# Fourteen late normalisations of a projection, spread over three pairs of heads, their low halves on GpSimd, and the output weights loaded and split in another order

## The chip, the cores and the metric

The kernel runs on one core of one Trainium2 chip. The metric is the device time of one execution in microseconds (us), the median of several runs. The engines of the core are TensorE (PE), VectorE (DVE), ScalarE (ACT), GpSimd (POOL) and SyncE (SP), which issues all DMAs. Each engine works through its own instruction list in order; semaphores make one wait for another.

## The reference

One transformer layer on x of shape (4, 512, 512): a batch of B = 4 sequences of T = 512 tokens. 32 query heads and 8 key/value heads of size 64, a sliding window of 256, and then a gated feed-forward part. All is float32.

```
xq = _rms_norm(x @ wq.T, q_norm_w, EPS)      # 2048 columns: 32 heads
xk = _rms_norm(x @ wk.T, k_norm_w, EPS)      # 512 columns: 8 heads
xv = x @ wv.T
...
scores = einsum('bhtd,bhsd->bhts', xq, xk) * scale + bias[None]   # bias: alibi slope * distance, -inf outside the window
attn = softmax(scores)
out = einsum('bhts,bhsd->bhtd', attn, xv)
return out @ wo.T
...
x = x + _layernorm(attention(_layernorm(x)))
x = x + _layernorm(feed_forward(_layernorm(x)))
```

## The kernel before

Matrix products are done on split operands: a float32 value is kept as a high half (rounded) and a low half (the rest), and a product is the sum of three. So each tensor that TensorE reads needs a rounding (ScalarE, a copy into the high half) and a subtraction (the low half).

**Stage 1, projections.** Four batches one after another. For a batch there are 16 blocks of query rows and 4 of key rows, 128 rows by 512 tokens each, numbered f = 0 to 19 (f 16 to 19 are the keys), kept in `raw[:, f]`. A block is normalised in three steps: VectorE scales it by its weight and the inverse root (line 927, `raw<-raw,norm_w,inv_rms`), ScalarE rounds it into `qk[:, f % 4, 0]` (line 731), VectorE subtracts (line 922, `split_raw`) into `qk[:, f % 4, 1]`. SP then stores the block to `q_scr` or `k_scr` (`store_qk`, line 385). The first LATE = 6 blocks are normalised in the batch's own time; the other 14 (f 6 to 19) are late: those of batches 0 to 2 are done during the next batch, those of the last batch during the first part of stage 2.

**Stage 2, attention.** 16 pairs n of key/value heads, four pairs to a batch. A pair is 32 units u: two key/value heads (u 0 to 15, and 16 to 31), four query tiles of 128 tokens in each, four query heads in each tile. The window of a tile is 128, 256, 384 and 384 wide, so units 0 to 3 and 16 to 19 are narrow, 4 to 7 and 20 to 23 are 256 wide, the rest 384. The stages of a unit run on a software pipeline whose lags stand in `LAGS`. In step u, VectorE does the subtraction for the transposed probabilities of unit u - 3 (line 997, `pT_lo`), then adds the bias to the scores of unit u (line 990, `u_sb`); ScalarE takes the exponentials of unit u (line 794) and rounds the transposed probabilities of unit u - 2 (line 802); TensorE makes scores (1231), transposes (1240) and the products with the values (1256 to 1258). Once for a group of four units (group g of a pair is units 4g to 4g+3), VectorE inverts the sums (line 1005, in step 4g+4) and takes the group's result out of PSUM into `o_raw` (line 1011, in step 4g+8).

GpSimd finishes a group (`finish_o`): it multiplies by the inverse sums into `o_mid` (line 598) and by the norm of v into `o_out` (line 604), which SP stores to `o_scr` (`store_o`, line 414). GpSimd also builds the next bias tile (`make_bias`, line 588), two for a pair. `o_raw` and `inv_sum` are rings of two, so VectorE waits before the inversion and the taking of a group until `o_mid` of the group two earlier is done:

```
def invert_sums(n, u):
    a = 2 * TT * n + u // REP
    dve.wait_ge(p_ready, UNITS * n + u + 1)
    at_least(dve, o_mid_ready, a - 1)
```

In pair 0, units 0 to 13 are each followed by one late normalisation of the last batch: in the loop of each engine, `norm(B - 1, u + LATE)` stands behind the unit's work, where VectorE scales block u + 6 and subtracts block u + 5, and ScalarE rounds block u + 5.

In pairs 1 to 4 the output weights are brought in: SP loads a quarter of them (1 MB, `load_wo`, line 433), and GpSimd rounds and subtracts four chunks of it (`split_wo`, lines 612 and 615), one behind groups 1 and 2 each and one behind groups 4 and 5 each. From pair 5 on each pair also carries one tile of the output projection: SP loads the tile (`load_o`, line 420) once the stores of the four pairs before have landed, and TensorE transposes it from step 4 on.

The order of all work is written out by hand, the same for each engine: `attention_loops` calls `attend(n)` for the 16 pairs, pair 0 and pair 5 written out, the others in loops of the engines.

## Time and profile before

| what | value |
|---|---|
| median of 3 runs | 1305.19 us (1304.18 to 1307.57) |
| the profiled execution's own time | 1309.66 us |
| its span in the trace | 1307.9 us |
| mean granted clock of TensorE, share of full speed | 0.973 |
| busy: PE, DVE, ACT, POOL | 93%, 73%, 58%, 28% of the span |

The median is of runs without a profile. The profiled execution is one run of its own; its time is the span plus 1.8 us that lie around it. In rows of busy time by stretch, the columns are: the stretch (us from the span's start), its length, busy us and count of instructions for PE, PE's weight loads (PEld), DVE, ACT and POOL, then the granted clock of TensorE (1.00 is 2.4 GHz, 0.50 is 1.2 GHz), the busy share of the DMA engines, and GB/s. In rows of a timeline the columns are: start in us, length in us, engine, line, operation, operands with their shapes, count, and in square brackets the idle time before it and what ended it. Matmul ends are modelled, so a busy PE need not be a PE at its peak.

### The profile page before, as it was taken

What the parts mean: (1) busy time and instruction counts of PE and PEld (TensorE: products, weight loads), DVE (VectorE), ACT (ScalarE), POOL (GpSimd) and SP (SyncE); (2) the same over time, 40 slices, a digit from 0 to 9 for tenths busy, and PEclk for the clock granted to TensorE, in tenths of its full rate; (3) what the DMA queues carried; (4) which work ended last, traced back from release to release, by engine and by line L of the source; (5) the groups of instructions that cost most, each with busy time, mean ns of one, the idle gap of its engine ahead of it and who ended that gap; (6) DMA issues with size and microseconds to landing.
All of it is one profiled execution on the core that took longest, in us unless ns stands there. A gap on an engine that the chain in (4) does not pass through costs nothing.

```text
span 1307.9 us, 30500 instructions
## 1 busy us (share of the span) xinstructions
PE 1214.9 (93%) x9016; PEld 1019.5 (78%) x9016; DVE 954.1 (73%) x2528; ACT 761.1 (58%) x2013; POOL 369.1 (28%) x445
## 2 busy tenths in 40 slices
PE   5999999996699998999999999999989979999998
PEld 4868777784577777898888888888877768888876
DVE  4597776858889987888888888888864346546464
ACT  3545455554589887777877777777732234232330
POOL 1000000001147766445354444434421100202021
PEclk9999999997599998999999999999989989999999
DMA  4216262455555556455454554545352252101010
GB/s 155 103 73 242 114 240 113 193 213 186 232 178 170 168 168 197 130 187 166 155 181 148 187 163 154 174 152 186 126 183 97 88 185 81 65 33 65 33 65 34
DMA packets 99245, 189.03 MB, mean 145 GB/s; under 512 B 8032, under 2 KB 36832, under 8 KB 99168
## 3 DMA queue, kind: packets, MB, share of 16 engines
q1 hardware_dynamic: 99168, 188.07, 42.2%
q8 instruction: 40, 0.66, 0.2%
q14 instruction: 37, 0.30, 0.1%
HBM read 116.48 MB, written 71.57 MB: 144 GB/s over the span
## 4 chain that ended last, share of the span: by engine, by line
PE 63%; DVE 12%; issue 10%; DMA 6%; ACT 4%; POOL 3%; SPq 1%; DVEq 1%; POOLq 0%; ACTq 0%
PE bank L1209 17%; PE bank L1340 15%; PE bank L1277 12%; PE bank L1240 6%; PE bank L1231 6%; DVE u_sb L990 3%; DMA wo_stage<-woT 2%; PE bank L1266 2%; DVE pT_lo L997 2%; DVE inv_rms L944 2%; ACT p_sb L794 1%; PE bank L1256 1%; PE bank L1258 1%; PE bank L1257 1%; DMA o_in<-o_scr 1%
## 5 line engine op out<-in xcount | busy, mean ns | idle before, releaser
L794 ACT ACTIVATE p_sb<-u_sb,low 128x384 f32<-128x384 f32 (+2 forms) x512 | 273.8, 535 | 84.6 <-DVE low L990 57.3
L990 DVE CUSTOM_DVE_ANT_0 u_sb<-bank,bias 128x384 f32<-128x384 f32 (+2 forms) x512 | 231.5, 452 | 40.5 <-PE bank L1231 21.0
L1231 PE MATMUL bank<-k_st,q_st 128*128 128x384 f32 (+2 forms) x1024 | 252.9, 329 | 6.5 <-DVE v_out L964 2.9
L1240 PE MATMUL bank<-ident,p_sb 128*128 128x128 f32 x1152 | 225.6, 287 | 31.4 <-DVE pT_lo L997 23.1
L997 DVE TENSOR_TENSOR pT_lo<-bank,pT_hi 128x384 f16<-128x384 f32 (+2 forms) x512 | 232.0, 453 | 28.9 <-ACT pT_hi L802 18.0
L802 ACT ACTIVATE pT_hi<-bank 128x384 f16<-128x384 f32 (+2 forms) x512 | 204.2, 399 | 49.5 <-PE bank L1240 47.7
L1231 PEld LDWEIGHTS bank<-k_st,q_st 128*128 128x128 f32 x1024 | 178.7, 195 | 30.3 <-DVE low L990 4.3
L1240 PEld LDWEIGHTS bank<-ident,p_sb 128*128 128x128 f32 x1152 | 139.8, 143 | 78.0 <-ACT p_sb L794 40.1
L598 POOL TENSOR_TENSOR o_mid<-o_raw,inv_sum 128x256 f32<-128x256 f32 x128 | 82.9, 648 | 285.1 <-DVE o_raw L1011 283.8
L561 POOL TENSOR_TENSOR rstd<-var_eps,minus_half 128x1 f32<-128x1 f32 (+1 forms) x31 | 23.4, 754 | 492.1 <-DVE var_eps L888 492.1
L1256 PE MATMUL bank<-v_st,pT_hi 128*128 128x64 f16 x1152 | 156.9, 195 | 0.5 <-DVE pT_lo L997 0.5
L1257 PE MATMUL bank<-v_st,pT_hi 128*128 128x64 f16 x1152 | 156.7, 194 | 0.0
L1258 PE MATMUL bank<-v_st,pT_lo 128*128 128x64 f16 x1152 | 156.7, 194 | 0.0
L1340 PE MATMUL bank<-zT_hi,gu 128*128 128x512 f32 x352 | 139.5, 396 | 0.6 <-DVE hid L1125 0.6
L1340 PE MATMUL bank<-zT_lo,gu 128*128 128x512 f32 x352 | 138.2, 393 | 0.0
L1209 PE MATMUL bank<-xT_hi,w_hi 128*128 128x512 f32 x320 | 127.5, 398 | 4.5 <-DVE xT_lo L906 4.5
L1209 PE MATMUL bank<-xT_hi,w_lo 128*128 128x512 f32 x320 | 125.1, 391 | 0.0
L1209 PE MATMUL bank<-xT_lo,w_hi 128*128 128x512 f32 x320 | 125.1, 391 | 0.0
L1277 PE MATMUL bank<-wo_hi,oT_hi 128*128 128x512 f32 x256 | 110.3, 431 | 8.9 <-DVE oT_lo L1016 8.9
L588 POOL TENSOR_TENSOR bias<-dist,slopes 128x1536 f32<-128x1536 f32 x33 | 91.1, 2762 | 87.5 <-PE bank L1209 87.5
L1256 PEld LDWEIGHTS bank<-v_st,pT_hi 128*128 128x128 f16 x1152 | 113.8, 101 | 1.7 <-DVE pT_lo L997 0.7
L1257 PEld LDWEIGHTS bank<-v_st,pT_hi 128*128 128x128 f16 x1152 | 107.5, 99 | 6.6
(114 smaller groups left out, 2416.5 us busy)
## 6 DMA issues: line engine op xcount, KB each, us to landing
...
o_scr<-o_out SPq DMA_DIRECT2D x128, 128.0 KB, 2.7
...
```

What stands on the lines that cost most here:

```text
L794: nc.scalar.activation(p_sb[:, u % RING, 0:w], u_sb[:, u % RING, 0:w], ACT.Exp, scale=-1.0, bias=low[:, u % RING:u % RING + 1], accum_out= ...
L802: nc.scalar.activation(pT_hi[:, u % RING, 0:w], bank[2 + u % 2][:, 0:w], ACT.Copy).then_inc(pT_hi_ready, 1)
L990: nc.vector.tensor_tensor_reduce(out=u_sb[:, u % RING, 0:w], in0=bank[u % 2][:, 0:w], in1=bias[:, 2 * u // UNITS, u % REP, at:at + w], sca ...
L997: nc.vector.tensor_tensor(pT_lo[:, u % RING, 0:w], bank[2 + u % 2][:, 0:w], pT_hi[:, u % RING, 0:w], ALU.subtract).then_inc(pT_ready, 1)
L1209: mm = nc.tensor.matmul(bank[n % 4][:], lhs, rhs, start=(kc == 0 and k == 0), stop=(kc == KC - 1 and k == 2))
L1231: mm = nc.tensor.matmul(bank[u % 2][:, 0:w], q_st[:, s, r, P * i:P * i + P], k_st[:, s, part, P * key:P * key + w], start=(part == 0), sto ...
L1240: mm = nc.tensor.transpose(bank[2 + u % 2][:, P * j:P * j + P], p_sb[:, u % RING, P * j:P * j + P], ident[:])
L1256: nc.tensor.matmul(acc, hi, v_hi, start=(j == 0), stop=False, skip_group_check=True)
L1257: nc.tensor.matmul(acc, hi, v_lo, start=False, stop=False, skip_group_check=True)
L1258: mm = nc.tensor.matmul(acc, lo, v_hi, start=False, stop=(j == tiles - 1), skip_group_check=True)
L1277: mm = nc.tensor.matmul(acc[:], lhs, rhs, start=(chunk == 0 and k == 0), stop=(chunk == QC - 1 and k == 2))
L1340: mm = nc.tensor.matmul(acc, lhs, rhs, start=(first and k == 0), stop=(last and k == len(products) - 1))
```

## The change

The 14 late blocks of the last batch move from units 0 to 13 of pair 0 to units 2, 4, 6, 18 and 20 of pairs 0, 1 and 2: f 6 to 10 in pair 0, f 11 to 15 in pair 1, f 16 to 18 at units 2, 4, 6 and f 19 at unit 18 of pair 2. VectorE keeps only the scaling (`scale_raw`). ScalarE rounds a block one unit later. The subtraction goes to GpSimd (`split_late`): for the blocks of a pair's first half it stands behind the bias of the second head and ahead of group 0, for those of the second half behind the next pair's bias and ahead of group 4. SP stores the late blocks in pieces (`store_late`), and the load of output weights is issued ahead of the pair's late stores. Two of the four splits of output weights in a pair move from behind groups 1 and 2 to behind groups 2 and 3. Pairs 1 to 4 are written out in place of a loop of the engines.

```
+LATE_UNITS = (2, 4, 6, 18, 20)
+LATE_NORMS = {}
+for _k, _f in enumerate(range(LATE, QC + KVC)):
+    LATE_NORMS[_k // len(LATE_UNITS), LATE_UNITS[_k % len(LATE_UNITS)]] = _f
+
+def late_norms(n, first, end):
+    return [LATE_NORMS[n, u] for u in LATE_UNITS if isinstance(n, int) and first <= u < end and (n, u) in LATE_NORMS]
...
 def attention_loops(eng, attend):
-    attend(0)
-    with eng.Fori(1, LAG) as n:
+    for n in range(LAG):
         attend(n)
...
 # SP
+            def store_late(n, first, end):
+                for f in late_norms(n, first, end):
+                    store_qk(B - 1, f)
+                    if f == QC + KVC - 1:
+                        stage1_stored(B)
...
                 load_heads(n, 0)
                 store_o(n - 1, 0, [TT - 1])
+                if isinstance(n, int):
+                    store_late(n - 1, UNITS // 2, UNITS)
...
                 if wo:
                     load_wo(n - 1)
+                if isinstance(n, int):
+                    store_late(n, 0, UNITS // 2)
                 store_o(n, 0, [0])
...
-            for f in range(LATE, QC + KVC):
-                store_qk(B - 1, f)
-            stage1_stored(B)
+            store_late(0, 0, UNITS // 2)
             store_o(0, 0, range(TT - 1))
-            with sp.Fori(1, LAG) as n:
+            for n in range(1, LAG):
                 attend(n, wo=True)
...
 # GpSimd
+            def split_late(n, first, end):
+                for f in late_norms(n, first, end):
+                    pool.wait_ge(qk_hi_ready, (QC + KVC) * (B - 1) + f + 1)
+                    pool.wait_ge(qk_ready, (QC + KVC) * (B - 1) + f)
+                    nc.gpsimd.tensor_tensor(out=qk[:, f % QK_RING, 1], in0=raw[:, f], in1=qk[:, f % QK_RING, 0].bitcast(F32),
+                                            op=ALU.subtract).then_inc(qk_ready, 1)
...
                 make_bias(n, q, 1)
+                split_late(n, 0, UNITS // 2)
                 for i in range(TT):
                     finish_o(n, q, 0, i)
-                    if wo and i in (1, 2):
-                        split_wo(n - 1, i - 1)
+                    if wo and i in (2, 3):
+                        split_wo(n - 1, i - 2)
...
                 make_bias(n + 1, q + 1, 0)
+                split_late(n, UNITS // 2, UNITS)
                 for i in range(TT // 2):
                     finish_o(n, q, 1, i)
...
 # ScalarE
-                    if isinstance(n, int) and n == 0 and u + LATE < QC + KVC:
-                        norm(B - 1, u + LATE)
+                    if isinstance(n, int) and n == 0 and u == 0:
+                        round_raw(B - 1, LATE - 1)
+                    for f in late_norms(n, u - 1, u):
+                        round_raw(B - 1, f)
...
 # VectorE
-                    if isinstance(n, int) and n == 0 and u + LATE < QC + KVC:
-                        norm(B - 1, u + LATE)
+                    if isinstance(n, int) and n == 0 and u == 0:
+                        split_raw(B - 1, LATE - 1)
+                    for f in late_norms(n, u, u + 1):
+                        scale_raw(B - 1, f)
```

The next rows are the instruction list of VectorE in pair 0, from the bias of unit 3 on, before the change. The `ISA` rows are the bias addition and the reading of its minimum; `pT_lo` is the subtraction of unit u - 3.

```order
L990 ISA u_sb,low<-bank,bias 128x128
L990 ISA low 128x1
L927 SCALAR_TENSOR_TENSOR raw<-raw,norm_w,inv_rms 128x512
L922 TENSOR_TENSOR qk<-raw,qk 128x512
L997 TENSOR_TENSOR pT_lo<-bank,pT_hi 128x128
L990 ISA u_sb,low<-bank,bias 128x256
L990 ISA low 128x1
L1005 RECIPROCAL inv_sum<-p_sum 128x4
L927 SCALAR_TENSOR_TENSOR raw<-raw,norm_w,inv_rms 128x512
L922 TENSOR_TENSOR qk<-raw,qk 128x512
L997 TENSOR_TENSOR pT_lo<-bank,pT_hi 128x128
L990 ISA u_sb,low<-bank,bias 128x256
```

The same place after the change:

```order
L1026 ISA u_sb,low<-bank,bias 128x128
L1026 ISA low 128x1
L1033 TENSOR_TENSOR pT_lo<-bank,pT_hi 128x128
L1026 ISA u_sb,low<-bank,bias 128x256
L1026 ISA low 128x1
L1041 RECIPROCAL inv_sum<-p_sum 128x4
L959 SCALAR_TENSOR_TENSOR raw<-raw,norm_w,inv_rms 128x512
L1033 TENSOR_TENSOR pT_lo<-bank,pT_hi 128x128
L1026 ISA u_sb,low<-bank,bias 128x256
L1026 ISA low 128x1
L1033 TENSOR_TENSOR pT_lo<-bank,pT_hi 128x128
L1026 ISA u_sb,low<-bank,bias 128x256
```

Each unit had a scaling and a subtraction of a late block; now unit 3 has neither and unit 4 has a scaling only.

The list of GpSimd in the loop of pairs 1 to 4 before, from the bias of the second head (`bias`) over groups 0 and 1 to the first split of output weights (`REGISTER_ALU` and `ISA` rows are loop arithmetic):

```order
L588 TENSOR_TENSOR bias<-dist,slopes 128x1536
L595 REGISTER_ALU
L598 TENSOR_TENSOR o_mid<-o_raw,inv_sum 128x256
L146 ISA
L604 ISA
L604 TENSOR_TENSOR o_out<-o_mid,v_norm 128x256
L595 REGISTER_ALU
L598 TENSOR_TENSOR o_mid<-o_raw,inv_sum 128x256
L604 TENSOR_TENSOR o_out<-o_mid,v_norm 128x256
L610 REGISTER_ALU
L612 ISA
L612 COPY wo_hi<-wo_stage 128x512
```

The list of GpSimd in pair 1 after, from the same bias on:

```order
L607 TENSOR_TENSOR bias<-dist,slopes 128x1536
L642 TENSOR_TENSOR qk<-raw,qk 128x512 x3
L617 TENSOR_TENSOR o_mid<-o_raw,inv_sum 128x256
L623 TENSOR_TENSOR o_out<-o_mid,v_norm 128x256
L617 TENSOR_TENSOR o_mid<-o_raw,inv_sum 128x256
L623 TENSOR_TENSOR o_out<-o_mid,v_norm 128x256
L617 TENSOR_TENSOR o_mid<-o_raw,inv_sum 128x256
L623 TENSOR_TENSOR o_out<-o_mid,v_norm 128x256
L631 CAST wo_hi<-wo_stage 128x512
L634 TENSOR_TENSOR wo_lo<-wo_stage,wo_hi 128x512
L617 TENSOR_TENSOR o_mid<-o_raw,inv_sum 128x256
L623 TENSOR_TENSOR o_out<-o_mid,v_norm 128x256
```

Three subtractions of late blocks (`qk<-raw,qk`) stand between the bias and group 0, and the split of output weights, which stood behind group 1, stands behind group 2.

The list of SyncE behind the last load of the projections before, over pair 0 and up to its leaving of pair 0:

```order
L385 DMA q_scr<-qk 128x1024
L467 DMA v_norm<-vn_scr 128x512
L468 DMA v_norm<-vn_scr 128x128
L385 DMA q_scr<-qk 128x1024 x10
L385 DMA k_scr<-qk 128x1024 x4
L414 DMA o_scr<-o_out 128x256 x3
```

The same place after, down to the last store ahead of the load of output weights (`k_st`, `q_st`, `v_st` are the loads of a head):

```order
L395 DMA q_scr<-qk 128x1024 x3
L424 DMA o_scr<-o_out 128x256 x3
L408 DMA k_st<-k_scr 64x1024 x2
L410 DMA q_st<-q_scr 128x4x512
L412 DMA v_st<-v_scr 128x512
L424 DMA o_scr<-o_out 128x256
L395 DMA q_scr<-qk 128x1024 x2
L424 DMA o_scr<-o_out 128x256 x3
L408 DMA k_st<-k_scr 64x1024 x2
L410 DMA q_st<-q_scr 128x4x512
L412 DMA v_st<-v_scr 128x512
L424 DMA o_scr<-o_out 128x256
```

All 14 late stores stood ahead of the first store of an attention result; now 3 of them do, 2 stand between stores and head loads, and the load of output weights (`wo_stage`) comes next, with 5 of the 14 issued.

## Rows read from the trace of the kernel before

**Rows 1.** The page of the profile, part 1: busy time, share of the span and instructions by engine.

```profile
PE 1214.9 (93%) x9016; PEld 1019.5 (78%) x9016; DVE 954.1 (73%) x2528; ACT 761.1 (58%) x2013; POOL 369.1 (28%) x445
```

**Rows 2.** Busy time by engine in pair 0 (its two halves), pair 2 and pair 4; columns as named in section 3.

```profile
319.16:357.77 38.61, 24.24 (x134) 17.99 (x135) 31.69 (x81) 21.67 (x61) 3.86 (x4) 0.50 0.66 255
357.77:374.50 16.73, 16.35 (x189) 13.50 (x188) 14.33 (x57) 13.95 (x48) 8.05 (x9) 0.94 0.51 156
...
406.32:438.18 31.86, 30.40 (x356) 24.63 (x354) 29.26 (x113) 28.59 (x97) 22.98 (x26) 1.00 0.53 173
...
471.24:505.14 33.90, 31.41 (x363) 26.25 (x362) 29.43 (x113) 28.41 (x95) 23.61 (x27) 0.95 0.50 159
```

**Rows 3.** Timeline of VectorE in pair 0, units 8 and 9: start, length, line, operands, [idle before].

```profile
337.44 0.55 DVE L990 CUSTOM_DVE_ANT_0 u_sb<-bank,bias 128x384 f32<-128x384 f32 x1
...
340.34 0.54 DVE L990 CUSTOM_DVE_ANT_0 u_sb<-bank,bias 128x384 f32<-128x384 f32 x1
340.81 0.08 DVE L990 DVE_READ_ACCUMULATOR2_ANT low<- 128x1 f32 x1
...
342.18 0.69 DVE L922 TENSOR_TENSOR qk<-raw,qk 128x512 fp32r<-128x512 f32 x1 [0.63 <-ACT qk L731]
```

**Rows 4.** Timeline of VectorE in pair 2: first operation of units 4, 8, 12, 16.

```profile
409.86 0.43 DVE L990 CUSTOM_DVE_ANT_0 u_sb<-bank,bias 128x256 f32<-128x256 f32 x1
...
413.26 0.55 DVE L990 CUSTOM_DVE_ANT_0 u_sb<-bank,bias 128x384 f32<-128x384 f32 x1
...
417.62 0.55 DVE L990 CUSTOM_DVE_ANT_0 u_sb<-bank,bias 128x384 f32<-128x384 f32 x1
...
422.14 0.28 DVE L990 CUSTOM_DVE_ANT_0 u_sb<-bank,bias 128x128 f32<-128x128 f32 x1
```

**Rows 5.** Timeline of TensorE in pair 0: transposes of two units in succession, clock at half.

```profile
355.76 0.87 PE L1240 MATMUL bank<-ident,p_sb 128*128 128x128 f32 x3 [1.38 <-DVE pT_lo L997]
...
357.39 0.86 PE L1240 MATMUL bank<-ident,p_sb 128*128 128x128 f32 x3
```

**Rows 6.** Two microseconds in which the clock of TensorE rises; columns as in group 2.

```profile
358.00:360.00 2.00, 2.00 (x26) 1.89 (x23) 1.33 (x7) 0.96 (x4) 1.21 (x2) 0.56 0.23 71
```

**Rows 7.** Timeline of GpSimd at the end of the projections.

```profile
296.85 5.90 POOL L588 TENSOR_TENSOR bias<-dist,slopes 128x1536 f32<-128x1536 f32 x2 [87.54 <-PE bank L1209]
```

**Rows 8.** Timeline of VectorE at the same time.

```profile
300.06 3.23 DVE L956 TENSOR_TENSOR sum_sq<-sum_sq,square 128x512 f32<-128x512 f32 x1
```

**Rows 9.** Line 956 of VectorE over the whole span: shortest, median and longest duration in ns.

```profile
L956 DVE TENSOR_TENSOR sum_sq<-sum_sq,square x72: 682/692/3228, 28.7 to 300.1; 128x512 f32<-128x512 f32 x72
```

**Rows 10.** Timeline of GpSimd in pairs 1 and 2.

```profile
394.65 0.61 POOL L612 CAST wo_hi<-wo_stage 128x512 f32 x1
395.51 1.28 POOL L615 TENSOR_TENSOR wo_lo<-wo_stage,wo_hi 128x512 f32 x1 [0.25 <-POOL wo_hi L612]
396.75 0.61 POOL L598 TENSOR_TENSOR o_mid<-o_raw,inv_sum 128x256 f32<-128x256 f32 x1
...
398.26 2.75 POOL L588 TENSOR_TENSOR bias<-dist,slopes 128x1536 f32<-128x1536 f32 x1
...
412.34 2.75 POOL L588 TENSOR_TENSOR bias<-dist,slopes 128x1536 f32<-128x1536 f32 x1
```

**Rows 11.** Timeline of GpSimd in pair 4: the first split of the fourth load.

```profile
489.52 0.61 POOL L612 CAST wo_hi<-wo_stage 128x512 f32 x1 [4.41 <-DMA wo_stage<-woT]
```

**Rows 12.** Timeline of VectorE in pairs 4 and 5: two long waits.

```profile
492.26 0.18 DVE L1005 RECIPROCAL inv_sum<-p_sum 128x4 f32<-128x4 f32 x1 [1.52 <-POOL o_mid L598]
...
511.45 0.42 DVE L990 CUSTOM_DVE_ANT_0 u_sb<-bank,bias 128x256 f32<-128x256 f32 x1 [1.99 <-PE bank L1231]
```

**Rows 13.** Timeline of SyncE's DMA issues around the start of pair 5.

```profile
493.87 1.17 SPq L398 DMA_DIRECT2D k_st<-k_scr  x2
...
496.77 0.35 SPq L414 DMA_DIRECT2D o_scr<-o_out  x1
504.17 0.38 SPq L420 DMA_DIRECT2D o_in<-o_scr  x1
```

More of the change, by code:

```diff
@@ L646, in _ @@
             make_bias(0, 0, 1)
+            split_late(0, 0, UNITS // 2)
             pool.wait_ge(vn_loaded, 2 * DMA)
@@ L650, in _ @@
             make_bias(1, 1, 0)
+            split_late(0, UNITS // 2, UNITS)
             for i in range(TT // 2):
                 finish_o(0, 0, 1, i)
-            with pool.Fori(1, LAG) as n:
+            for n in range(1, LAG):
                 attend(n, n, wo=True)
@@ L922, in split_raw, with scale_raw @@
                 nc.vector.tensor_tensor(qk[:, f % QK_RING, 1], raw[:, f], qk[:, f % QK_RING, 0].bitcast(F32), ALU.subtract).then_inc(qk_ready, 1)
-            def norm(b, f):
+            def scale_raw(b, f):
                 dve.wait_ge(inv_ready, 2 * b + f // QC + 1)
@@ L928, in norm @@
                                                ALU.mult, ALU.mult).then_inc(scaled, 1)
+            def norm(b, f):
+                scale_raw(b, f)
                 if f:
```

## The prediction

> **What bounds the kernel now.** I read the page first, then the timelines of VectorE and ScalarE where the late blocks lie, and then busy time cut at the first bias addition of each pair. TensorE is busy 93% of the span [rows 1], but the cut shows a place where it is not. The first 16 units of pair 0 take 38.61 us, with the granted clock at 0.50 (1.2 GHz) throughout and TensorE busy 24.2 us of them; the next 16 units take 16.73 us at 0.94. Pair 2, with no late blocks, takes 31.86 us at 1.00, with VectorE busy 29.3 and ScalarE 28.6 of it; pair 4 takes 33.90 [rows 2]. Pair 3, which lies between the end of pair 2 at 438.18 and the start of pair 4 at 471.24, takes 33.06.
>
> Why pair 0 is slow stands in its timeline. Unit 8 starts at 337.44 and unit 9 at 340.34, a period of 2.90 us. In it VectorE adds the bias, scales a block (0.74), then stands idle 0.63 us for ScalarE's rounding (`ACT qk L731`) before it subtracts (0.69) [rows 3]. ScalarE can't round earlier, since its exponential for the unit is ahead. So it is a serial round trip for each block. The same eight units 8 to 15 in pair 2 take 422.14 - 413.26 = 8.88 us, 1.11 each [rows 4]. TensorE starves meanwhile and its clock stays at the lower level.
>
> Three later places matter. In pair 4, GpSimd waits 4.41 us for the load of output weights, with group 2 queued behind the split; VectorE then stands 1.52 us at an inversion of sums that needs `o_mid` [rows 11, 12]. At step 5 of pair 5 VectorE stands 1.99 us for TensorE, which is waiting for `o_in`, whose load was issued at 504.17 [rows 12, 13].
>
> **The change, part by part.** All in us. An offset is a time from a pair's first bias addition.
>
> *Pair 0, first half: from 38.6 to about 22.* Eleven of 14 scalings and 14 of 15 subtractions leave it, and with them the round trips; block 5's subtraction at unit 0 stays, with its wait. Units 1 to 7 become narrow units with three scalings. What limits them is TensorE at half clock: two successive sets of transposes, with three sets of value products and one 128-wide pair of scores between, start 357.39 - 355.76 = 1.63 apart [rows 5]. Scaled by width, I estimate 0.85 for a 128-wide unit, 1.3 for a 256-wide one and 1.9 for a 384-wide one (1.63 plus the wider scores). Unit 0, 2.0; units 1 to 3 with a scaling, 3.3; units 4 to 7 with two, 5.7: unit 8 at 11.0 to 11.5. Before, it came at 337.44 - 319.16 = 18.3. Units 8 to 15 take 8.9 at full clock. TensorE had been without long waits from 355.8 when the clock rose between 358 and 360 [rows 5, 6], so I expect it back within two units of unit 8, at 0.8 extra each: 10.5. Sum 22, a gain of 16.6; the ends are 26.5 (clock down to unit 16, 1.9 each) and 19.5.
>
> *Pair 0, second half: from 16.7 to 17.6.* The cold start, 0.9, goes (15.8 in pair 2: 422.14 - 406.32); two scalings come, 0.66 each (0.74 long, less the 0.07 or 0.08 by which an operation overlaps the next: 340.34 + 0.54 against 340.81 [rows 3]), and 0.5 for collisions on GpSimd. Net for pair 0: -15.7.
>
> *Scalings in pairs 1 and 2: +5.9.* Nine at 0.66. VectorE and ScalarE are each some nine tenths busy there, so a scaling lands on the path; the rounding (0.5) lies beside it on ScalarE. The lower bound is nothing, if waits of VectorE take it in; the upper is the 1.6 it cost in pair 0 ((38.61 - 15.8) / 14).
>
> *A scaling that meets GpSimd: +4.7 over pairs 1 and 2.* A scaling reads two SBUF operands, as does line 956, which lasts 0.69 in the median but 3.23 once, at 300.06, just when GpSimd ran two bias tiles from 296.85 to 302.75 [rows 7 to 9]. It ended 0.54 behind the second tile. So one waits for the other to finish. The Trainium skill's page "SBUF — State Buffer", section "SBUF: two separate sides", has it as an exclusive lock between GpSimd and a VectorE operation with two SBUF inputs; by this rule the trace agrees, and it speaks against this change. By the row the sum below is -8.0; if the row of 3.23 had another cause it would be -12.7. Where do they meet? GpSimd's bias of the second head started at 412.34, offset 6.0, and lasts 2.75 [rows 10]. With two scalings ahead of it the bias runs from 6.7 to 9.4, and the scaling of unit 6 comes at about 7.4: 2.0 of wait. The bias additions and `pT_lo` read PSUM and are not held. The other scalings meet shorter work, 0.2 each or so: 2.4 in pair 1, 2.3 in pair 2.
>
> *GpSimd's queue: +2.4.* A split of output weights costs 396.75 - 394.65 = 2.10, its subtraction of the late blocks' size 1.28, a group 398.26 - 396.75 = 1.51, a bias 2.75 [rows 10]. Pair 1 needs 2 x 2.75 + 8 x 1.51 + 4 x 2.10 + 5 x 1.3 = 32.5 of GpSimd in about 38. It fits, but not everywhere. Behind the taking of group 3 (step 20) now stand group 3, a split, a bias, two subtractions and `o_mid` of group 4: 1.5 + 2.1 + 2.75 + 2.6 + 0.8 = 9.8. VectorE wants that `o_mid` at the inversion in step 28. Steps 20 to 28 take 417.62 - 409.86 = 7.76 (of the same widths) [rows 4] and one scaling: 8.4. VectorE stands some 1.5 in pair 1; in pair 2, with one subtraction and no scaling there, 0.9. In pair 0 there is no split and no wait. In the first half of a pair the same sum with three subtractions is 1.5 + 2.75 + 3.9 + 0.8 = 9.0 against 7.8 + 1.3 + the 2.0 of the lock, so nothing more. Ends: 0, and 6 if the lock delays GpSimd too.
>
> *Pairs 3 to 5: -5.3.* The first split now comes behind group 2, at offset 15.8 + 2.7 = 18.5; the weights landed at 489.52 - 471.24 = 18.3 at the latest [rows 11]. GpSimd's wait, and VectorE's, go: pair 3 from 33.06 and pair 4 from 33.90 to 31.85, 3.3 in all. Group 2 of pair 4 is then finished some 3 us earlier, so head loads (issued 493.87, 22.6 into the pair, where step 20 of pair 2 comes near 19.4 by the same steps [rows 4]) and the store that the load of `o_in` waits for (496.77) go out that much earlier, and `o_in` lands near step 4 of pair 5: I take 2.0 off. Lower bound none, if that store's 7.2 us behind the head loads are what counts.
>
> *Moved or added at nothing.* Late stores: 0.5 MB each, 14 of them, in pairs where DMA engines are half busy [rows 2]; head loads have 12 units of lead. A store ahead of a group's store makes that up to 2 us later, with a ring of four in `o_out`. Pairs 1 to 4 written out: pair 0 was so already, and a loop's turn shows no gap to gain.
>
> Sum: -15.7 + 5.9 + 4.7 + 2.4 - 5.3 = -8.0. From the profiled execution's 1309.66 that is 1301.7; that run lies 4.5 above the median of 1305.19, so for a median I forecast 1297.2.
>
> **The rivals.**
>
> *GpSimd is hardly felt* (0.16). Lock and queue cost 1, since VectorE's delays slide past GpSimd's work: -15.7 + 5.9 + 1 - 5.3 = -14, 1291. For it: the schedule leaves GpSimd 5 us in pair 1. Against: the bias lies just where unit 6's scaling comes.
>
> *The gain is given back* (0.20). The clock stays low to unit 16 (+4.5), and stalls in pairs 1 and 2 cost 3 more with a short spell at half clock, as in pair 4 (0.95 there [rows 2]): -0.5 to -3, 1303. For it: with TensorE busy 24.2 of 38.6 us, 63%, the clock did not rise [rows 2].
>
> *Slower, by the lock* (0.08). If each of the nine scalings of pairs 1 and 2 meets a bias or a split and waits 2 us or more on average, these pairs cost 5.9 + 18 + 2.4 = 26.3, against 15.7 and 3.3 (with `o_in` not better): +7, 1312. It decides from 1.9 us of average wait on. Against: GpSimd's operations other than bias last 0.6 to 1.3 [rows 10].
>
> *The forecast* (0.56): -4 to -12, 1293 to 1301.
>
> **How the numbers follow.** Within 0.3% (3.9 us) is what a measurement of this kernel can't tell from none. Faster takes the forecast's and the first rival's chance, 0.72; same the second, 0.20; slower 0.08. The range leaves out the slower case and a tenth at the low end: 1288 to 1305.
>
> **What the profile will show.** Right: unit 16 of pair 0 about 22 us after unit 0, the clock at 1.00 from about unit 10; a scaling of 2.7 us beside a bias tile in pairs 1 and 2; an inversion waiting for `o_mid` in step 28 of pair 1; pairs 1 and 2 near 39.4 and 37.8 (6 to 7.6 more); pair 4 at 31.9. Wrong: a clock at 0.50 to the end of pair 0, a wait at a group other than 4, pairs of 34 (no lock) or above 42, or `o_in` landing as late as before.

## The result and the profile after

The changed kernel takes 1291.52 us in the median (1289.15 to 1292.30), the kernel before 1306.38 in runs of the same session: a ratio of 0.9876, 95% interval 0.9859 to 0.9893. The ratios in this document are estimates over the single runs of both kernels, and not exactly the quotient of two medians, which is 0.9886 here. By the medians the change takes 14.9 us off. The forecast was 1297.2; the forecast, too, was below the time before, but by 8.0. The profiled executions are 1309.66 and 1292.3, and their spans 1307.9 and 1290.5.

The page's busy time by engine, to be held against [rows 1]: VectorE has lost 10.0 us, GpSimd has gained 20.3, and TensorE has the same instructions at a higher mean clock (0.989 after, 0.973 before).

```profile
PE 1202.0 (93%) x9016; PEld 1009.0 (78%) x9016; DVE 944.1 (73%) x2514; ACT 758.4 (59%) x2013; POOL 389.4 (30%) x459
```

Busy time of the changed kernel, cut at the first bias addition of each pair (the two halves of pair 0, then pairs 1 to 5), which answers to [rows 2]:

```profile
317.01:334.36 17.35, 15.31 (x145) 12.51 (x146) 15.32 (x57) 15.08 (x49) 6.81 (x7) 0.83 0.72 255
334.36:351.51 17.15, 15.43 (x179) 12.24 (x178) 15.59 (x60) 15.16 (x51) 10.95 (x11) 1.00 0.60 193
351.51:389.26 37.75, 30.93 (x355) 24.48 (x354) 32.88 (x118) 30.73 (x102) 29.27 (x29) 1.00 0.62 214
389.26:425.12 35.86, 30.97 (x356) 24.64 (x354) 31.98 (x117) 30.37 (x102) 30.30 (x31) 1.00 0.61 214
425.12:456.09 30.97, 30.12 (x353) 24.41 (x352) 28.60 (x112) 28.13 (x97) 23.12 (x27) 1.00 0.55 180
456.09:487.41 31.32, 30.32 (x355) 24.54 (x354) 28.78 (x113) 28.24 (x97) 23.35 (x27) 1.00 0.57 184
487.41:527.67 40.26, 39.35 (x413) 35.39 (x412) 34.10 (x121) 32.41 (x102) 18.91 (x21) 1.00 0.59 189
```

| length of | before | forecast | after |
|---|---|---|---|
| pair 0, units 0 to 15 | 38.61 | 22 | 17.35 |
| pair 0, units 16 to 31 | 16.73 | 17.6 | 17.15 |
| pair 1 | 31.82 | 39.4 | 37.75 |
| pair 2 | 31.86 | 37.8 | 35.86 |
| pair 3 | 33.06 | 31.85 | 30.97 |
| pair 4 | 33.90 | 31.85 | 31.32 |
| pair 5 | 42.32 | 40.3 | 40.26 |

Summed over the table the change takes 17.6 us off. Pair 6 gives back 0.4 (41.20 to 41.62) and pairs 7 to 14 another 0.4. Pair 0 starts 2.15 earlier in the profile of after; in the profiles of the other kernels below it starts anywhere from 316.70 to 318.98 with nothing changed ahead of it, so that is not the change's. Behind the start of pair 15, where no kernel here differs, 1.6 are lost (390.05 before, 391.67 after). So from the start of pair 0 to the end of the span the two profiles differ by 15.2. The stretch behind the start of pair 15 takes 388.28 to 391.67 in the fourteen profiles, and it tends to be shorter where the clock of TensorE stood at 1.2 GHz for less of it: up to the last 3 us of the span that is 10.2 us in e6's profile (388.35), 13.7 in before's and 17.1 in after's. Spans of single profiles can therefore differ by up to 3.4 us for this alone, and the kernels below are compared by the lengths of their pairs and by medians.

**Pair 0.** The clock of TensorE in stretches of 2 us from the span's 318 on:

```profile
318.00:320.00 2.00, 1.02 (x6) 0.70 (x5) 1.62 (x6) 1.03 (x5) 0.00 (x0) 0.50 0.99 354
320.00:322.00 2.00, 2.00 (x15) 1.87 (x14) 1.87 (x9) 1.98 (x8) 0.31 (x1) 0.50 1.04 347
322.00:324.00 2.00, 2.00 (x17) 1.80 (x16) 1.99 (x8) 1.71 (x7) 1.36 (x2) 0.76 1.05 276
324.00:326.00 2.00, 1.63 (x19) 1.13 (x19) 1.86 (x9) 1.93 (x8) 1.21 (x1) 1.00 1.02 383
```

TensorE is busy without a gap in the second and third rows, at 1.2 GHz, and goes to 2.4 GHz inside the third: at unit 6, not two units behind unit 8. Unit 8 starts at 8.23 (forecast 11.0 to 11.5), and units 8 to 15 take 9.12 (forecast 10.5).

**Pairs 1 and 2.** VectorE (first fence) and GpSimd (second fence) in these pairs:

```profile
357.74 0.96 DVE L959 SCALAR_TENSOR_TENSOR raw<-raw,norm_w,inv_rms 128x512 f32<-128x512 f32 x1
...
366.08 0.18 DVE L1041 RECIPROCAL inv_sum<-p_sum 128x4 f32<-128x4 f32 x1 [1.06 <-POOL o_mid L617]
...
385.19 0.18 DVE L1041 RECIPROCAL inv_sum<-p_sum 128x4 f32<-128x4 f32 x1 [1.45 <-POOL o_mid L617]
...
403.66 0.18 DVE L1041 RECIPROCAL inv_sum<-p_sum 128x4 f32<-128x4 f32 x1 [1.07 <-POOL o_mid L617]
...
420.89 0.18 DVE L1041 RECIPROCAL inv_sum<-p_sum 128x4 f32<-128x4 f32 x1 [0.83 <-ACT p_sb L825]
```

```profile
356.22 1.00 POOL L617 TENSOR_TENSOR o_mid<-o_raw,inv_sum 128x256 f32<-128x256 f32 x1 [2.16 <-DVE o_raw L1047]
357.42 0.73 POOL L623 TENSOR_TENSOR o_out<-o_mid,v_norm 128x256 f32<-128x256 f32 x1 [0.20 <-DVE low L1026]
358.10 3.20 POOL L607 TENSOR_TENSOR bias<-dist,slopes 128x1536 f32<-128x1536 f32 x1
361.27 4.13 POOL L642 TENSOR_TENSOR qk<-raw,qk 128x512 fp32r<-128x512 f32 x3
365.35 0.62 POOL L617 TENSOR_TENSOR o_mid<-o_raw,inv_sum 128x256 f32<-128x256 f32 x1
...
384.46 0.62 POOL L617 TENSOR_TENSOR o_mid<-o_raw,inv_sum 128x256 f32<-128x256 f32 x1
...
420.17 0.61 POOL L617 TENSOR_TENSOR o_mid<-o_raw,inv_sum 128x256 f32<-128x256 f32 x1
```

The scaling of unit 6 starts 0.36 ahead of the bias tile, and the tile doesn't hold it: it ends 2.60 ahead of the tile's end. What holds it a little, to 0.96 in place of 0.75, is the `o_out` that began at 357.42. There are four waits for `o_mid`, at steps 12 and 28 of each pair: an inversion starts 0.11 behind the end of each `o_mid` shown. The last wait is named after ScalarE, but `o_mid` ends at 420.78, and the inversion follows by the same 0.11. The waits add up to 1.06 + 1.45 + 1.07 + 0.83 = 4.4. I had forecast 1.5 and 0.9 at the two steps 28, and nothing at the two steps 12.

**Pairs 3 to 5.** GpSimd's first split of pair 4, and SyncE's issues around it, which answer to [rows 11, 13]:

```profile
474.37 0.61 POOL L631 CAST wo_hi<-wo_stage 128x512 fp32r<-128x512 f32 x1 [0.15 <-DMA wo_stage<-woT]
```

```profile
474.61 1.12 SPq L408 DMA_DIRECT2D k_st<-k_scr  x2
...
484.95 0.38 SPq L430 DMA_DIRECT2D o_in<-o_scr  x1
```

The 4.41 of waiting in pair 4 became 0.15. Head loads go out 18.5 into the pair (before: 22.6), and the load of `o_in` 2.46 ahead of pair 5 (before: 0.97).

### The profile page after: what moved, and what is told of

Its sections match the earlier page's. It is cut to its first block, busy times and chain, and to the rows that moved or that the text cites. A ratio compares the mean times of both kernels' runs of the same rounds, so it can differ in the third digit from the quotient of the medians.

```text
span 1290.5 us, 29717 instructions
## 1 busy us (share of the span) xinstructions
PE 1202.0 (93%) x9016; PEld 1009.0 (78%) x9016; DVE 944.1 (73%) x2514; ACT 758.4 (59%) x2013; POOL 389.4 (30%) x459
## 4 chain that ended last, share of the span: by engine, by line
PE 70%; DVE 12%; issue 8%; ACT 4%; POOL 3%; DMA 2%; DVEq 0%; ACTq 0%; POOLq 0%; SPq 0%
PE bank L1247 17%; PE bank L1378 17%; PE bank L1315 12%; PE bank L1278 8%; PE bank L1269 7%; DVE u_sb L1026 3%; ACT p_sb L825 2%; PE bank L1294 2%; PE bank L1304 2%; PE bank L1296 2%; PE bank L1295 2%; DVE pT_lo L1033 2%; DVE inv_rms L980 2%; POOL bias L607 1%; POOL qk L642 1%
## 5 line engine op out<-in xcount | busy, mean ns | idle before, releaser
L1269 PE MATMUL bank<-k_st,q_st 128*128 128x384 f32 (+2 forms) x1024 | 247.2, 323 | 4.4 <-DVE v_out L1000 2.9
L1278 PE MATMUL bank<-ident,p_sb 128*128 128x128 f32 x1152 | 220.9, 282 | 29.1 <-DVE pT_lo L1033 19.2
L1269 PEld LDWEIGHTS bank<-k_st,q_st 128*128 128x128 f32 x1024 | 175.4, 191 | 27.7 <-DVE v_out L1000 3.3
L1278 PEld LDWEIGHTS bank<-ident,p_sb 128*128 128x128 f32 x1152 | 137.1, 141 | 75.9 <-ACT p_sb L825 49.9
L1294 PE MATMUL bank<-v_st,pT_hi 128*128 128x64 f16 x1152 | 154.7, 193 | 0.5 <-DVE pT_lo L1033 0.5
L1295 PE MATMUL bank<-v_st,pT_hi 128*128 128x64 f16 x1152 | 154.9, 193 | 0.0
L1294 PEld LDWEIGHTS bank<-v_st,pT_hi 128*128 128x128 f16 x1152 | 112.3, 100 | 1.7 <-DVE pT_lo L1033 0.7
L1295 PEld LDWEIGHTS bank<-v_st,pT_hi 128*128 128x128 f16 x1152 | 105.9, 98 | 5.8
```

Of the source, the lines that this page charges most:

```text
L1269: mm = nc.tensor.matmul(bank[u % 2][:, 0:w], q_st[:, s, r, P * i:P * i + P], k_st[:, s, part, P * key:P * key + w], start=(part == 0), sto ...
L1278: mm = nc.tensor.transpose(bank[2 + u % 2][:, P * j:P * j + P], p_sb[:, u % RING, P * j:P * j + P], ident[:])
L1294: nc.tensor.matmul(acc, hi, v_hi, start=(j == 0), stop=False, skip_group_check=True)
L1295: nc.tensor.matmul(acc, hi, v_lo, start=False, stop=False, skip_group_check=True)
```

## The experiments

All times are medians; each ratio is to the kernel before, timed in the same session. Lengths of pairs and single instructions are from one profile of each kernel.

| kernel | us | ratio, 95% interval |
|---|---|---|
| changed | 1291.52 | 0.9876 [0.9859, 0.9893] |
| e1 written out | 1303.42 | 0.9970 [0.9955, 0.9984] |
| e2 and split order | 1300.45 | 0.9955 [0.9939, 0.9971] |
| e3 spread, subtraction on VectorE | 1308.36 | 1.0007 [0.9997, 1.0017] |
| e4 pair 0 only, subtraction on GpSimd | 1300.84 | 0.9953 [0.9937, 0.9970] |
| e5 old split order | 1291.71 | 0.9884 [0.9865, 0.9903] |
| e6 groups ahead of late blocks | 1287.13 | 0.9848 [0.9828, 0.9869] |
| e7 scaling meets bias | 1293.72 | 0.9898 [0.9880, 0.9917] |
| e8 GpSimd's subtraction cut | 1285.95 | 0.9841 [0.9821, 0.9861] |
| e9 VectorE's scaling cut | 1285.70 | 0.9842 [0.9823, 0.9861] |
| e10 splits behind 2, 4, 5, 6 | 1287.89 | 0.9859 [0.9836, 0.9882] |
| e11 group 0 ahead only | 1289.22 | 0.9868 [0.9845, 0.9892] |
| e12 six, four, four | 1287.20 | 0.9848 [0.9826, 0.9870] |

### e1 and e2: the other parts of the change, alone

To the kernel before, e1 does only this, on each engine (GpSimd's lines are shown), and e2 adds the order of the splits:

```
-            with pool.Fori(1, LAG) as n:
+            for n in range(1, LAG):
...
 # e2 as well
-                    if wo and i in (1, 2):
-                        split_wo(n - 1, i - 1)
+                    if wo and i in (2, 3):
+                        split_wo(n - 1, i - 2)
```

> The kernel before, with pairs 1 to 4 written out in place of a loop, and nothing else. The trace of the changed kernel has pairs 3 and 4 at 31.0 and 31.3 us, less than the 31.8 of pair 2 before, where no wait stood to be removed. Theory A: a written-out pair is 0.5 to 0.9 us shorter than one in a loop, so 2 to 3.5 us less than before. Theory B (my prediction's): a loop costs nothing, the kernel is at before's time, and what pairs 3 and 4 gained is all from the order of the splits.

> As the run before it, and two of the four splits of output weights behind groups 2 and 3 in place of 1 and 2. The late blocks stay as before. Theory A: the waits of GpSimd for the load and of VectorE for o_mid in pairs 3 and 4 go (3.3 us), and o_in is in time in pair 5 (2 us): 5 us less than the written-out kernel, 7 to 8.5 less than before. Theory B: only the split waits go and pair 5 still waits for its load, 3 us less than the written-out kernel.

Pair 4 of e1, and of e2:

```profile
466.67:500.88 34.21, 31.20 (x355) 26.30 (x354) 29.23 (x113) 28.72 (x97) 24.04 (x29) 0.95 0.50 163
```

```profile
465.55:497.03 31.48, 30.34 (x355) 24.57 (x354) 28.82 (x113) 28.29 (x97) 23.26 (x27) 1.00 0.64 207
```

Pairs 1 to 4 take 130.64 before (374.50 to 505.14 [rows 2]), 128.96 in e1 and 125.02 in e2. So writing out brings 1.7 there, where I had nothing, and the split order 3.9, where I had 3.3 for the waits. Pair 2, in which VectorE waits for no `o_mid` in either kernel, is 31.86 before and 31.13 in e1. Only some of this is the same in each pair: the first four units take 3.30 in all four pairs of e1, and 3.43 to 3.55 before. Pair 1 falls by 0.2 alone, and pair 4 grows by 0.3, since GpSimd waits 4.90 there for the weights and VectorE 2.05 for `o_mid`. Pair 5, which is not in the loop, falls from 42.32 to 41.01 in e1: its `o_in` is issued 1.55 ahead of the pair, where it was 0.97. e2 brings it to 40.39. So a part of what I had put down to the split order comes with the writing out. Which instructions of the loop cost the time was not taken apart. In both kernels theory A came, in e1 with somewhat more than its 2 to 3.5. In e1 the clock falls in pair 4 as it did before; in e2, with the wait gone, it doesn't.

### e3: the spread without GpSimd

The changed kernel, with the subtraction on VectorE two units behind the scaling:

```
-                split_late(n, 0, UNITS // 2)
...
+                    for f in late_norms(n, u - 2, u - 1):
+                        split_raw(B - 1, f)
```

> The changed kernel, with the 14 late blocks spread the same way but the subtraction kept on VectorE, two units behind the scaling, so that the rounding is done by then. Theory A: 14 subtractions at 0.6 us cost VectorE 8.4, of which the three waits for o_mid in pairs 1 and 2 (1.06, 1.45 and 1.07 us) are given back: 4 to 5 us slower than the changed kernel, 1296. Theory B: GpSimd's share is a loss, through its queue and the shared port: not slower than the changed kernel, 1291 or less.

This kernel has all other parts of the change, those of e2 with them. Against e2's 1300.45 the spread with VectorE's subtractions costs 7.9: pairs 0 to 2 take 40.85, 43.60 and 39.33, 123.8 together, against 117.4 in e2 (55.08, 31.12, 31.19) and 108.1 in the changed kernel. What pair 0 gains, 14.2, pairs 1 and 2 lose and more, 20.6. The spread by itself does most of the work where it was meant to: the first half of pair 0 takes 20.03 here, 38.61 before and 17.35 in the changed kernel. But with the subtractions on VectorE, where this kernel puts them, pairs 1 and 2 lose it all again. Neither theory had this: A expected 4 to 5 us over the changed kernel, and it is 17. In pair 1 VectorE (first fence) meets GpSimd (second), and TensorE starves (third, a stretch of 4 us):

```profile
366.39 2.11 DVE L943 TENSOR_TENSOR qk<-raw,qk 128x512 fp32r<-128x512 f32 x1 [0.65 <-ACT qk L750]
```

```profile
365.21 2.75 POOL L607 TENSOR_TENSOR bias<-dist,slopes 128x1536 f32<-128x1536 f32 x1
```

```profile
366.00:370.00 4.00, 2.10 (x11) 1.56 (x11) 3.61 (x6) 1.51 (x6) 1.95 (x1) 0.50 1.03 337
```

A subtraction of 0.69 takes 2.11, and TensorE, busy 2.10 of 4.00 us, stands at 1.2 GHz. The clock had already fallen at 365.09, ahead of this meeting, and it falls once in each half of pairs 1 and 2. The subtraction also waits 0.65 for its rounding, so the round trip is not gone either. How much of the 20.6 is the subtractions' own length, how much the meetings and how much the clock isn't separated, and a place for them on VectorE that is clear of GpSimd was not tried.

### e4: GpSimd without the spread

The kernel before, with the 14 blocks where they were and their subtractions on GpSimd:

```
-                        norm(B - 1, u + LATE)
+                        norm(B - 1, u + LATE, late=True)     # VectorE: scaling only
...
+            split_late(range(6, 13))                         # GpSimd, ahead of group 0
...
+                split_late({0: range(13, 17), 1: range(17, 20)}.get(i, ()))
```

> The kernel before, with all 14 late blocks in units 0 to 13 of pair 0, but the subtraction on GpSimd; loop and order of splits as before. Theory A: the cost in pair 0 is the round trip from VectorE over ScalarE back to VectorE, so that without it a unit falls from 2.9 us to TensorE's 1.9 at half clock: 10 to 12 us less than before, 1295, and spreading is worth the few us that are left. Theory B: the clock is what matters and it stays at half as long as all blocks stand in pair 0, with GpSimd's 14 subtractions holding group 0 back: at most 6 us less, 1300 or more.

The number is theory B's, and so is the clock in part: it stands at 1.2 GHz for the first 17.1 us of the pair, to unit 10. Pair 0 falls from 55.34 to 47.60, about a third of what the whole change takes off it. Four microseconds of the 47.60 are a wait of another kind, shown by TensorE and by SyncE:

```profile
364.32 0.68 PE L1242 MATMUL bank<-k_st,q_st 128*128 128x128 f32 x2 [4.08 <-DMA q_st<-q_scr]
```

```profile
322.76 17.62 SPq L385 DMA_DIRECT2D q_scr<-qk  x10
341.72 6.34 SPq L385 DMA_DIRECT2D k_scr<-qk  x4
352.26 1.31 SPq L414 DMA_DIRECT2D o_scr<-o_out  x3
353.95 1.16 SPq L398 DMA_DIRECT2D k_st<-k_scr  x2
```

All late stores stand ahead of the head loads in SyncE's list, so a faster pair 0 runs into them. The changed kernel, which stores in pieces, shows no wait for heads. I had counted the pieces at nothing. That they guard a pair 0 of 34.50 from such a wait is likely by e4, but the changed kernel with all stores in one piece wasn't tried.

### e5: the old split order in the changed kernel

```
-                    if wo and i in (2, 3):
-                        split_wo(n - 1, i - 2)
+                    if wo and i in (1, 2):
+                        split_wo(n - 1, i - 1)
```

> The changed kernel (1291.5 us), with the splits of output weights back behind groups 1 and 2. Theory A (the split order is worth what it was worth alone, 3.0 us from 1303.42 to 1300.45): GpSimd again waits for the weights behind group 1, in pairs 3 and 4 above all, and 1294 to 1296, ratio to the kernel before about 0.9905. Rival B (in the changed kernel the load of weights is issued ahead of the late stores, which alone brings them in time): 1291 to 1292. Rival C (the two splits behind group 1 and 2 also lie in the way of o_mid in pairs 1 and 2, where late subtractions stand ahead of them): 1297 or more, with waits of VectorE for o_mid above 1.1 us at steps 12 and 16 of pair 1.

The number, 1291.71, is rival B's, but not for its reason: the weights don't come in time. GpSimd waits again, and VectorE waits in pair 5:

```profile
472.18 0.61 POOL L631 CAST wo_hi<-wo_stage 128x512 fp32r<-128x512 f32 x1 [3.67 <-DMA wo_stage<-woT]
```

```profile
493.01 0.42 DVE L1026 CUSTOM_DVE_ANT_0 u_sb<-bank,bias 128x256 f32<-128x256 f32 x1 [1.80 <-PE bank L1269]
```

Pair 4 is 0.8 longer (32.10) and pair 5 1.9 longer (42.15), as the forecast's account of these waits has it; but pair 1 is 0.7 and pair 2 0.8 shorter (37.01, 35.06), since group 3 is then no longer followed by a split ahead of `o_mid` of group 4, and the waits at the two steps 28 are gone. The new order moves the wait of pairs 4 and 5 to pairs 1 and 2; 2.7 against 1.5 by these lengths, and no difference in the medians.

### e6, e11, e10 and e12: the order on GpSimd

e6 puts groups 0 and 4 ahead of the late subtractions in pairs 1 and 2, e11 group 0 only. Pair 0 is written apart in GpSimd's list and keeps its order in all four kernels:

```
-                split_late(n, 0, UNITS // 2)
                 for i in range(TT):
                     finish_o(n, q, 0, i)
+                    if i == 0:
+                        split_late(n, 0, UNITS // 2)
```

e10 is e6 with the splits behind groups 2, 4, 5 and (in the next pair) 6. e12 is e6 with six, four and four late blocks in pairs 0, 1 and 2:

```
-LATE_UNITS = (2, 4, 6, 18, 20)
+LATE_UNITS = (2, 4, 6, 18, 20, 22)
+LATE_NORMS = dict(zip([(_n, _u) for _n, _c in enumerate((6, 4, 4)) for _u in LATE_UNITS[:_c]],
+                      range(LATE, QC + KVC)))
```

> The changed kernel, with GpSimd finishing group 0 ahead of the three late subtractions and group 4 ahead of the two. Theory A (VectorE's waits for o_mid in the changed kernel, 1.06 and 1.45 in pair 1 and 1.07 in pair 2, are the price of GpSimd's order): they go, the later groups have room (step 8 to the inversion of step 16 is 8.9 us, GpSimd needs 6.0 of it), and the time is 1288 (1287 to 1289.5), ratio about 0.985. Rival B (these waits only take in time that VectorE would lose elsewhere, at TensorE or at the lock): 1291 to 1292. Rival C (the late subtractions now run later, beside other scalings and rounding, or delay group 5 past step 32): 1293 or more, with a wait for o_mid at the start of pairs 2 and 3.

> The changed kernel, with GpSimd finishing group 0 ahead of the three late subtractions, and the second half of each pair as it was. Theory A (the gain of 4.4 us by both moves is 1.06 and 1.07 at step 12 of pairs 1 and 2, and the rest at step 28): 1289.5 (1288.7 to 1290.2). Rival B (the second move only shifts its wait to the start of pair 2, so this one alone gives as much or more): 1287.5 or less. Rival C (a wait removed at step 12 comes back at step 28): 1291 or more.

> The kernel with groups 0 and 4 ahead of the late subtractions (1287.13 us), with GpSimd's four splits of output weights behind groups 2, 4, 5 and 6 (the last in the next pair) in place of 2, 3, 4 and 5. In that kernel pair 2 still starts late: VectorE waits 0.77 for o_mid at 387.30 and its scaling at 389.09 takes 1.59, and units 0 to 8 of pair 2 take 9.94 where they took 8.16 before; pair 3 is 0.36 longer than it was. Theory A (GpSimd needs 16.2 us from step 20 to the end of the pair, where some 14 are to be had, and 3.6 of them can go to its idle time at the start of the next pair, 2.85 and 2.16): both go, 1285 (1284.3 to 1286.3). Rival B (the split only meets other work there, and a scaling waits behind it): 1286.5 to 1288. Rival C (output weights ready too late for pair 5, or the next load held up): 1289 or more.

> The kernel with groups 0 and 4 ahead of the late subtractions (1287.13 us), with the 14 late blocks dealt out six to pair 0 (units 2, 4, 6, 18, 20, 22) and four each to pairs 1 and 2 (units 2, 4, 6, 18), in place of five, five and four. Pair 0 has no split of output weights, so GpSimd has room there; in pair 1 it is one subtraction of 1.3 us short, which in that kernel made pair 2 35.57 us long, with a scaling of 1.59 us at 389.09 and a clock of 0.90. Theory A (GpSimd's queue in the second half of pair 1 is what is left of its price): pair 0 35.2, pair 1 34.3, pair 2 34.0, 1285.3 (1284.5 to 1286.3). Rival B (the scaling at the start of pair 2 meets a split all the same): pair 2 stays at 35.3 or more, 1286.8 to 1288. Rival C (the sixth block in pair 0 makes it wait for late stores or at the inversion of step 28): pair 0 at 36.5 or more.

e6 is 1287.13, by the ratios 3.7 us and by the pairs 1 to 3 2.7 us faster than the changed kernel, and its four waits for `o_mid` at steps 12 and 28 are gone. Pair 1 is 34.97. But pair 2 stays at 35.57. VectorE (first fence), GpSimd (second) and pair 2 (third) in e6:

```profile
387.30 0.18 DVE L1043 RECIPROCAL inv_sum<-p_sum 128x4 f32<-128x4 f32 x1 [0.77 <-POOL o_mid L617]
...
389.09 1.59 DVE L961 SCALAR_TENSOR_TENSOR raw<-raw,norm_w,inv_rms 128x512 f32<-128x512 f32 x1
```

```profile
388.86 1.28 POOL L634 TENSOR_TENSOR wo_lo<-wo_stage,wo_hi 128x512 fp32r<-128x512 f32 x1 [0.18 <-POOL wo_hi L631]
```

```profile
386.24:421.81 35.57, 32.71 (x356) 27.37 (x354) 32.68 (x117) 30.50 (x102) 30.84 (x32) 0.90 0.65 222
```

GpSimd is late at the end of pair 1; its last split runs beside the first scaling of pair 2, which takes 1.59, and the clock falls at 390.78, just as that scaling ends, so that its mean over the pair is 0.90. e11 has no such meeting (pair 2 34.66) but keeps 1.46 of wait at step 28 of pair 1, and 1.19 in pair 5: 1289.22. e10 was to clear the meeting and only moved it, to unit 4:

```profile
393.22 1.74 DVE L963 SCALAR_TENSOR_TENSOR raw<-raw,norm_w,inv_rms 128x512 f32<-128x512 f32 x1
```

```profile
393.15 1.27 POOL L634 TENSOR_TENSOR wo_lo<-wo_stage,wo_hi 128x512 fp32r<-128x512 f32 x1 [0.18 <-POOL wo_hi L631]
```

In e12 pair 1 falls to 33.74 and pair 2 to 34.63, but pair 0 takes 35.95, with a new wait at step 28 (first row), and the meeting is still there (second row):

```profile
348.93 0.18 DVE L1042 RECIPROCAL inv_sum<-p_sum 128x4 f32<-128x4 f32 x1 [1.02 <-POOL o_mid L616]
...
388.97 1.60 DVE L960 SCALAR_TENSOR_TENSOR raw<-raw,norm_w,inv_rms 128x512 f32<-128x512 f32 x1
```

The intervals of e6, e10, e11 and e12 overlap, and which is best can't be said. e6's runs (1285.89 to 1288.35) lie all below the changed kernel's, though the intervals of the two ratios still touch. In e6 and e11 theory A came. In e10 and e12 mine fell: GpSimd's work behind step 20 met a scaling in both. For e12 this is no full trial, since its wait in pair 0 stands where three subtractions are still ahead of group 4; the same deal with group 4 ahead in pair 0 too wasn't tried.

### e7: a scaling that meets the bias tile

```
-LATE_UNITS = (2, 4, 6, 18, 20)
+LATE_UNITS = (2, 4, 7, 18, 20)
```

> The changed kernel, with the third scaling of each first half in unit 7 in place of unit 6, where it meets GpSimd's bias tile (358.10 for 3.20 us in pair 1). Theory A (lock: a VectorE operation with two SBUF inputs waits for GpSimd's): the scaling takes 2 to 3 us in place of 0.74 in pairs 0, 1 and 2, the late subtractions come 1 us later, and the wait at step 12 grows: +4 to +8, 1296 to 1299. Rival B (no lock on a scaling, only on other operations): it stays at 0.7 to 1.1 us, the wait at step 12 grows by 1 at most in two pairs, and the time is 1291 to 1293.5. Rival C (lock, but GpSimd starts its bias behind the scaling all the same): scaling 0.7 to 1.1 and the bias over 3.0, same time.

VectorE and GpSimd in pair 1:

```profile
359.54 0.42 DVE L1033 TENSOR_TENSOR pT_lo<-bank,pT_hi 128x256 f16<-128x256 f32 x1 [0.91 <-ACT pT_hi L833]
...
360.22 1.99 DVE L959 SCALAR_TENSOR_TENSOR raw<-raw,norm_w,inv_rms 128x512 f32<-128x512 f32 x1
```

```profile
358.92 2.75 POOL L607 TENSOR_TENSOR bias<-dist,slopes 128x1536 f32<-128x1536 f32 x1
```

A scaling of 0.75 takes 1.99, and 1.98 in pair 2. It ends at 362.21, 0.54 behind the bias tile's 361.67. The same 0.54 stands in e3 (368.50 against 367.96), in e6 (390.68 against 390.14), in e10 (394.96 against 394.42) and in [rows 7, 8]. It isn't a fixed tail of the lock. In e9, where the scaling has 8 columns, VectorE (first fence) ends 0.02 behind GpSimd (second):

```profile
371.91 0.55 DVE L959 SCALAR_TENSOR_TENSOR raw<-raw,norm_w,inv_rms 128x8 f32<-128x8 f32 x1
```

```profile
371.15 1.29 POOL L634 TENSOR_TENSOR wo_lo<-wo_stage,wo_hi 128x512 fp32r<-128x512 f32 x1 [0.18 <-POOL wo_hi L631]
```

In both cases that is the instruction's own length (0.75 and 0.22) less 0.2, as if nearly all of its work still lay before it when GpSimd ended. And it goes both ways: in the changed kernel the scaling came first (357.74 to 358.70), and the bias tile beside it took 3.20 in place of 2.75; the `o_mid` at 356.22, begun 0.22 behind the scaling of unit 4, took 1.00 in place of 0.62. The Trainium skill's page "SBUF — State Buffer", section "SBUF: two separate sides", says that whichever starts first has the shared ports for its whole instruction and the other stands; by that rule these traces agree. The theory's size was too large: pairs 0, 1 and 2 are 0.78, 1.12 and 1.09 longer and the time 2.2, not 4 to 8. Nor is this the price of the lock alone. Pair 0 has no bias tile beside unit 7, and is 0.78 longer all the same: at unit 6 VectorE now stands idle for ScalarE (0.81 there, 0.91 in the first row), time in which the changed kernel's scaling lay, and the scaling of unit 7 is added behind it. In pairs 1 and 2 the idle time and the 1.0 of the lock come to 1.9 each; against that a VectorE so late finds `o_mid` ready at step 12 and no longer waits its 1.06 there.

### e8 and e9: the price of the two halves of the work

> The changed kernel, with GpSimd's late subtractions cut to 8 of 512 columns, which leaves out most of the low halves of the 14 late blocks. It prices what these subtractions cost as work on GpSimd. Theory A (they cost VectorE's three waits for o_mid, 3.6 us, and some tenths each in operations that overlap them): 1287 (1286 to 1288.5), pairs 1 and 2 at 35.8 and 34.5. Rival B (GpSimd is hardly felt): 1290.5 or more, pairs unchanged. Rival C (contention reaches further than the waits show): 1284 or less.

> The changed kernel (1291.5 us), with VectorE's scaling of the late blocks cut to 8 of 512 columns, which leaves out most of their normalisation. It prices the scalings. Theory A (each of the nine in pairs 1 and 2 is worth about 0.66 to 0.74 us on VectorE's path, and the five in pair 0 the same, but GpSimd's queue then stands out by as much at steps 12 and 28): 14 x 0.7 less some 3 of longer waits, 1284 to 1287. Rival B (a scaling also costs by holding up TensorE and ScalarE, some 1 us or more each): 1281 or less. Rival C (the scalings lie in VectorE's idle time): 1289 or more.

The edits are `qk[:, f % QK_RING, 1, 0:8]` and its operands in GpSimd's subtraction, and `raw[:, f, 0:8]` and its operands in VectorE's scaling; e8 leaves out most of the late blocks' low halves, e9 most of their normalisation, and both serve as prices only. With the subtractions cut, pairs 1 and 2 take 34.97 and 33.70, 68.67 in all and 4.94 less than the changed kernel's 73.61; pair 0 stays at 34.50. With the scalings cut, pairs 0 to 2 take 33.32, 35.57 and 34.30, less by 1.18 and 3.74. e9's waits for `o_mid` are 0.71, 1.53, 0.76 and 0.90: at step 12 shorter than the changed kernel's by a third, at step 28 a little longer. The scalings don't vanish in e9: the nine in pairs 1 and 2 last 3.4 in all, where they last 8.0 in the changed kernel, since GpSimd still holds them. So the 3.74 is for 4.6 us of VectorE's work. Both kernels came out within theory A's range or 0.05 from it.

## Why the prediction was right, and where its sum was off

**Direction and main mechanism: right. Size: 17.6 in pairs 0 to 5, where the sum had 8.0.** The time fell by 14.9, since some 2.4 were lost again behind pair 5, most of them in code that the change doesn't touch. Of the 9.6 between sum and measurement 5.1 lie in pair 0, 3.1 in pairs 1 and 2, and 1.4 in pairs 3 to 5. By its own terms:

- *Pair 0, first half, 22*: mis-sized, 17.35. The steps to unit 8 were priced too high (8.23, not 11 and more), and the clock rose inside 322 to 324 and not about unit 10. Units 1 to 3 took 2.00 for a forecast 3.3, and units 4 to 7 took 4.25 for 5.7. The 5.7 was a slip besides: four units at 1.3 and two scalings at 0.74 make 6.7. The estimate scaled TensorE's period at half clock by width and put each scaling on top of it; in the rows from 320 to 324 both engines are full, VectorE 3.86 of 4.00 and TensorE 4.00, so a scaling lies beside TensorE's work there and not on top of it. This term alone is 4.7 of the difference. e3 and e4 show what it rests on: with the blocks spread and the subtractions left on VectorE the first half is 20.03, and with the subtractions moved but the blocks not spread it is 27.61.
- *Scalings, +5.9*: right. e8 against e2, which has no late blocks in these pairs, gives 68.67 - 62.31 = 6.4 for nine, with what they lose to short meetings with GpSimd in it.
- *A scaling that meets GpSimd, +4.7*: the mechanism was right, its place wrong. I put unit 6's scaling at offset 7.4 and the bias at 6.7; they came at 6.23 and 6.59, in the other order, and the cost was some 0.2 to the scaling and 0.45 to the bias tile. The short meetings were priced well, at 0.2 each: all nine scalings together last 8.0, 1.3 more than nine of 0.74 would. One unit later the scaling is held for 1.0 more (e7).
- *GpSimd's queue, +2.4*: mis-sized, 4.9 (e8). Step 28 was right in pair 1 (1.45 for 1.5) and in pair 2 (0.83 for 0.9). (The 0.9 was itself 0.2 above its own sum, 8.5 against 7.8.) Step 12 was held to have room, 9.0 of GpSimd against 11.1, with 2.0 of the lock's delay to VectorE in the 11.1. Without it the sum still has 9.1 against 9.0, a wait of nothing, and the waits were 1.06 and 1.07. VectorE was there after 8.9, as the sum had it (356.09 to 365.02). What was missing is that the lock works on GpSimd too: from the `o_mid` at 356.22 to the end of the one at 365.35 GpSimd took 9.75, not 9.0, with 0.4 of it in the first `o_mid` and 0.45 in the bias tile, each begun just behind a scaling. The forecast had named this as its upper end and put nothing into the sum for it. So the two terms were not apart: what the lock doesn't cost VectorE, the queue does. Together with the scalings they were to cost 13.0 and cost 11.3, held against e2. (The forecast lengths of pairs 1 and 2, 39.4 and 37.8, hold 0.5 more than its sum.)
- *Pairs 3 to 5, -5.3*: -6.7. The waits were right (e2: 3.9; pair 5 -2.06 for -2.0, and e5 shows it come back when `o_in` is issued 0.51 ahead of the pair and not 2.46). Missing was the writing out of the loop, which I had said brings nothing: e1 shows 1.7 in pairs 1 to 4 and 1.3 in pair 5.
- *The rivals.* "GpSimd is hardly felt" named 1291, the time that came, by a mechanism that did not: GpSimd costs 4.9. It is right by accident. The forecast's own range of 1288 to 1305 held although four of the five numbers in its sum were off, by 1.4 to 5.1, three of them towards a shorter time; in that the forecast was lucky. "The gain is given back" needed a low clock to unit 16; it rose ten units sooner. "Slower, by the lock" needed long waits for each scaling; it says from 1.9 on average, but by its own terms 1.2 is enough to reach the time before and 1.6 to be 3.9 above it. No scaling of late blocks took over 1.08, a wait of some 0.3.

The whole is not the sum of its parts. By the medians, writing out and split order are worth some 7, the spread on top of them with VectorE's subtractions costs 7.9, and with GpSimd's it gains 8.9 (1300.45 to 1291.52, two sessions; 10.3 by the ratios); GpSimd's taking over without the spread gains 7 from the kernel before (1307.82 to 1300.84 in one session).
